# Cross-attention and a low-rank FFN: the value products on half chunks of 64 keys

## The chip, the cores and the metric

The kernel runs on one core of one Trainium2 chip. The metric is the device time of one execution in microseconds, as the median of several runs; lower is better. The kernel before takes 623.55 us (three runs, 623.04 to 624.56). One more execution, with the hardware profiler on, took 620.38 us.

## The reference

Everything is float32. `x` has shape (2, 2048, 512), `ctx` (2, 77, 384): 4096 tokens attend to only 77 keys of their own batch entry.

```
def _L0_xattn_ref(query, key_value, Wq, bq, Wk, bk, Wv, bv, Wo, bo):   # 16 heads of 32
    q = (query @ Wq + bq) -> (B, H, Nq, 32);  k, v likewise from key_value
    attn = jnp.einsum('bhqd,bhkd->bhqk', q, k) * 32 ** -0.5
    attn = jax.nn.softmax(jnp.clip(attn, -10000.0, 10000.0), axis=-1)
    x = jnp.einsum('bhqk,bhkd->bqhd', attn, v).reshape(B, Nq, 512)
    return x @ Wo + bo
def _L0_ffn_ref(x, U1, V1, b1, U2, V2, b2):                            # rank 128, 2048 hidden
    return gelu(x @ U1 @ V1 + b1) @ U2 @ V2 + b2
x = x + _L0_xattn_ref(_layernorm(x), ctx_768, ...)
x = x + _L0_ffn_ref(_layernorm(x), ...)
```

## The kernel before, in words

Each engine has its own instruction stream, ordered by hand; semaphores connect them. The attention stage goes over NA = 16 blocks of TA = 256 tokens, each of two tiles of 128 tokens (u = 0, 1); the blocks take turns between the two batch entries (b = 0, 1). The FFN stage goes over NB = 8 blocks of 512 tokens. The first blocks of a stage and its last are written out in the instruction streams, the ones between run in a hardware loop (`pairs`, `eng.Fori`).

Large projections split each float32 operand into a high part in fp32r and a low part, the rest, and add three products of the parts (`product`, L929). ScalarE writes the high part, VectorE or GpSimd subtracts to get the low one. The smaller products of attention are plain float32.

In one turn of the attention loop, block n is at several stages at once. TensorE's order for a turn (its `body`) is, for u = 0 and then u = 1: scores of block n (`scores`, L977); the turn of the probabilities of block n-1, first eight of the ten chunks of 128 (`turn_probs`, L1003); one half of the query projection of block n+1 (`project_q`); the last two chunks; the output projection of block n-2 (`project_out`). Then, once per block: the turn of the normalised input z of block n+2 (`turn_z`, L951) and the value products of block n-1 (`weigh_values`, L1026).

The softmax of a tile passes through four engines. VectorE clips the scores out of PSUM into a row buffer of 16 heads x 77 = 1232 values (`clip`, L717) and takes the maxima (L726). GpSimd subtracts them (`subtract_max`, L390), ScalarE takes the exponent (`exponent`, L527), VectorE the sums and reciprocals (`sums`, L731, L733), GpSimd multiplies (`normalise`, L397). Then TensorE turns the row in chunks of 128 into banks B5 and B6, and ScalarE copies them to `pt` (L520). There are four row buffers `sc`, two for each block.

A head's 77 keys lie across the 128-wide chunks at any offset. So the value products go by `PIECES`, the 25 overlaps of a head with a chunk. For each of them `vrows` holds a 128-row matrix that is zero outside the piece's rows, filled once by 25 small copies on SP's queue (L276) behind a memset. A product has 128 rows and 32 columns (one head); four heads share a bank by four column tiles. The heads of the first two groups end in B5, those of the other two in B6. After each half, `pv_full` lets ScalarE copy the high part to `ot` (`heads_high`, L533) and VectorE subtract the low part (`heads_low`, L739).

VectorE's order for a turn (its `body`, L822 on) is: for u = 0, 1: clip and maxima of block n; for u = 1 also the sums of tile 0; for u = 0 the two normalised z of block n+2 (`norm_z`, L661); the addition of the projected output to x (`y_sum`, L749); the statistics of block n+3 (L650, L653). Then the low parts of z (`turned_z`, L669), the sums of tile 1, the low parts of the heads of block n-1 (`heads_low`, L739). The first two blocks have an order of their own, `first_blocks` (L796). ScalarE's order ends a turn with the high parts of z (L489), the exponent of tile 1 and `heads_high`. GpSimd has normalise of tile 1 of the block before, subtract_max, two additions of a bias to x (L406), subtract_max, normalise, and a small power for the statistics (L368, L371).

`turn_z` used bank B6 for u = 0 and B4 or B7 for u = 1. `turn_probs` waits for `heads_low` (`ot_lo`), since B5 and B6 hold the value products before.

Of the kernel before, what the change touches and what calls it, by code (L numbers as in the profile page):

```python
# [4 lines left out]
F32 = mybir.dt.float32  # L5
# [5 lines left out]
P = 128  # L11
# [17 lines left out]
PIECES = [(h, c) for h in range(H) for c in range(NCH) if c * P < (h + 1) * KV and (c + 1) * P > h * KV]  # L29


def head_at(q):

    return (q % G) * GH + q // G


NP = len(PIECES)
# [35 lines left out]
def pairs(eng, total, body):  # L73

    head, tail = (2, 2) if total > 8 else (1, 1)
    for j in range(head):
        body(j)
    with eng.Fori(head, total // 2 - tail) as j:
        body(j)
    for j in range(total // 2 - tail, total // 2 + 1):  # L80
        body(j)


def xattn_ffn(nc, x, ctx, wq, bq, wk, bk, wv, bv, wo, bo, u1, v1, b1, u2, v2, b2, out):
# [7 lines left out]
    with stack:  # L92
# [3 lines left out]
        def sem(name):  # L96
# [27 lines left out]
        ss = sb("ss", [P, 4 * NCH * P])  # L124
        sc = ss[:, :].rearrange("p (s w) -> p s w", s=4)
# [5 lines left out]
        vrows = sb("vrows", [P, B, NP, DH])  # L131
# [8 lines left out]
        v_f = once[0:KV, KC * B * KV:KC * B * KV + B * D].rearrange("p (b d) -> p b d", b=B)  # L140
# [31 lines left out]
        z_bank = lambda j, b, u: B6 if u == 0 else B7 if is_block(2, j, b) or is_block(3, j, b) else B4  # L172
# [18 lines left out]
        wq_hi, wq_lo, wq_lo_pool, wo_hi, wo_lo, pad_zero, bias_ready = (  # L191
            sem(n) for n in ("wq_hi", "wq_lo", "wq_lo_pool", "wo_hi", "wo_lo", "pad_zero", "bias_ready"))
# [29 lines left out]

        def piece_rows(h, c):

            first, end = max(h * KV, c * P), min((h + 1) * KV, (c + 1) * P)
            return first - c * P, first - h * KV, end - first
# [18 lines left out]
        def _(sp):  # L245
# [85 lines left out]
            pairs(sp, NA, body)  # L331
# [17 lines left out]
            pairs(sp, NB, body2)  # L349
# [5 lines left out]
        def _(pool):  # L355
# [19 lines left out]
            pool.memset(vrows[:, :, :, :], 0.0).then_inc(zeroed, 1)  # L375
# [8 lines left out]
            def heads(t, k):  # L384
                return t[:, k, 0:HKV].rearrange("p (h w) -> p h w", h=H)
# [258 lines left out]
        def _(dve):  # L644
# [62 lines left out]
            for k in range(4):  # L707
                last = dve.memset(sc[:, k, HKV:], 0.0)
# [523 lines left out]
```

## Time and profile before

| | us |
|---|---|
| median of three runs | 623.55 |
| the profiled execution | 620.38 |
| its span, first to last instruction | 618.4 |
| TensorE busy | 582.5 (94%) |
| VectorE busy | 495.8 (80%) |
| GpSimd busy | 356.3 (58%) |
| ScalarE busy | 310.5 (50%) |
| attention stage, first scores to last output projection | 29 to 366 |

The profile has one row per instruction. Views of it add these up by line, by waits, along the chain of work that ended last, or list them in order of time. PE is TensorE's matmul, PEld its weight load, DVE VectorE, ACT ScalarE, POOL GpSimd, SP the queue of loads and stores. L1026 is line 1026 of the kernel. A float32 matmul that is not fp32r stands as two records. In the chain of waits a PE piece ends where the next begins; in the timeline the modelled end of a matmul reaches past the start of the next.

### The profile page before, as it was taken

How to read it: one execution, taken by the hardware profiler on the slowest of the kernel's cores; microseconds unless marked ns; L12 is line 12 of the kernel's file. 1: busy time of each engine (PE TensorE's matmuls, PEld its weight loads, DVE VectorE, ACT ScalarE, POOL GpSimd, SP SyncE). 2: the span in 40 equal slices, each digit the busy share in tenths (PEclk: the TensorE clock that was granted, in tenths of full speed). 3: DMA queues.
4: the chain of work that ended last, by engine and by line, in shares of the span. 5: the costliest groups of instructions: out<-in, count | busy, mean ns of one | idle time of the engine just before them, and what ended most of it. 6: DMA issues, size and time to landing. Idle time of an engine off the chain costs nothing.

```text
span 618.4 us, 12409 instructions
## 1 busy us (share of the span) xinstructions
PE 582.5 (94%) x4583; PEld 474.5 (77%) x4583; DVE 495.8 (80%) x706; ACT 310.5 (50%) x505; POOL 356.3 (58%) x250
## 2 busy tenths in 40 slices
PE   7886999999999999999998999898989898989996
PEld 6685887888888888888876677686868686868774
DVE  3589779889888888889679887988888888887664
ACT  1344354444544444535464546656565565656562
POOL 1549656665756665665556465646464738283641
PEclk9999999999999999999999999999999999999999
DMA  8423082303231223112320421212121111201012
GB/s 268 143 66 105 20 272 88 93 29 101 85 102 41 78 88 99 57 64 69 120 70 35 136 56 64 79 59 68 69 69 69 63 56 39 97 17 52 18 51 85
DMA packets 29733, 50.10 MB, mean 81 GB/s; under 512 B 5069, under 2 KB 6783, under 8 KB 29567
## 3 DMA queue, kind: packets, MB, share of 16 engines
q1 hardware_dynamic: 29215, 48.80, 23.8%
q10 hardware_dynamic: 480, 0.80, 0.5%
q8 instruction: 24, 0.39, 0.3%
q14 instruction: 14, 0.11, 0.1%
HBM read 32.49 MB, written 16.78 MB: 80 GB/s over the span
## 4 chain that ended last, share of the span: by engine, by line
PE 70%; DVE 13%; issue 5%; ACT 4%; POOL 3%; DMA 3%; SPq 1%; DVEq 0%; ACTq 0%; POOLq 0%
PE bank L929 40%; PE ps_s L929 10%; PE bank L1026 6%; PE bank L1003 5%; PE ps_s L977 4%; DVE once L770 3%; PE bank L1050 2%; DMA ss<-in_L_xattn_Wv 2%; DVE hs_r L791 2%; DVE hs_r L793 2%; DVE ssum L731 2%; PE bank L951 1%; DVE smax L726 1%; DMA xs<-in_x 1%; DVE ss L717 1%
## 5 line engine op out<-in xcount | busy, mean ns | idle before, releaser
L464 POOL TENSOR_TENSOR hs_r<-ss,hs_r 128x512 fp32r<-128x512 f32 x63 | 84.4, 1340 | 107.1 <-ACT hs_r L631 107.0
L610 ACT ACTIVATE ss<-ps_s,bias_c 128x512 f32<-128x512 f32 x128 | 88.1, 689 | 83.2 <-PE ps_s L929 80.2
L929 PE MATMUL bank<-hs_r,u_r 128*128 128x512 f32 x384 | 111.0, 398 | 14.0 <-DVE hs_r L793 10.5
L390 POOL TENSOR_TENSOR ss<-ss,smax 128x1232 f32<-128x1232 f32 x32 | 75.1, 2346 | 70.0 <-DVE smax L726 69.9
L929 PE MATMUL ps_s<-p1t_r,v_r 128*128 128x512 f32 x384 | 112.4, 401 | 0.7 <-DVE p1t_r L782 0.7
L929 PE MATMUL bank<-zt_r,wqo_r 128*128 128x256 f32 x768 | 99.5, 285 | 0.4 <-DVE zt_r L669 0.4
L929 PEld LDWEIGHTS bank<-hs_r,u_r 128*128 128x128 f32 x384 | 70.9, 188 | 36.4 <-DVE hs_r L793 8.8
L929 PE MATMUL bank<-wqo_r,ot_r 128*128 128x512 f32 x384 | 97.7, 403 | 0.2 <-DVE xs L749 0.2
L929 PEld LDWEIGHTS bank<-zt_r,wqo_r 128*128 128x128 f32 x768 | 93.2, 189 | 1.6 <-issue 1.0
L397 POOL TENSOR_TENSOR ss<-ss,rsum 128x1232 f32<-128x1232 f32 x32 | 72.1, 2253 | 38.6 <-DVE rsum L733 38.6
L929 PEld LDWEIGHTS bank<-wqo_r,ot_r 128*128 128x128 f32 x384 | 69.8, 188 | 15.6 <-issue 0.6
L929 PEld LDWEIGHTS ps_s<-p1t_r,v_r 128*128 128x128 f32 x384 | 69.8, 188 | 15.5 <-DVE v_r L756 1.1
L520 ACT ACTIVATE pt<-bank 128x512 f32<-128x512 f32 (+1 forms) x96 | 48.2, 526 | 43.1 <-PE bank L1003 43.1
L497 ACT ACTIVATE qt<-bank,bias_c 128x256 f32<-128x256 f32 x64 | 26.9, 472 | 70.0 <-PE bank L929 70.0
L793 DVE TENSOR_TENSOR hs_r<-ss,hs_r 128x512 fp32r<-128x512 f32 x64 | 59.7, 933 | 2.2
L791 DVE CAST hs_r<-ss 128x512 fp32r<-128x512 f32 x64 | 45.5, 710 | 14.7 <-ACT ss L610 14.6
L1003 PE MATMUL bank<-ident,ss 128*128 128x128 f32 x320 | 49.1, 281 | 8.4 <-DVE ot_r L739 2.4
L749 DVE TENSOR_TENSOR xs<-bank,xs 128x512 f32<-128x512 f32 x32 | 22.0, 687 | 40.9 <-PE bank L929 40.9
L1026 PE MATMUL bank<-pt,vrows 128*32 128x256 f32 x800 | 51.8, 383 | 0.0
L527 ACT ACTIVATE ss<-ss 128x1232 f32<-128x1232 f32 x32 | 39.5, 1234 | 24.4 <-POOL ss L390 24.4
L731 DVE TENSOR_REDUCE ssum<-ss 128x16 f32<-128x1232 f32 x32 | 45.7, 1429 | 2.1 <-ACT ss L527 2.1
L726 DVE TENSOR_REDUCE smax<-ss 128x16 f32<-128x1232 f32 x32 | 45.8, 1432 | 1.0
(89 smaller groups left out, 861.5 us busy)
## 6 DMA issues: line engine op xcount, KB each, us to landing
xs<-in_x SPq DMA_DIRECT2D x64, 256.0 KB, 2.8
y_between<-xs SPq DMA_DIRECT2D x32, 256.0 KB, 2.0
xs<-y_between SPq DMA_DIRECT2D x4, 1024.0 KB, 5.6
fw<-y_between SPq DMA_DIRECT2D x4, 1024.0 KB, 5.6
out<-fw SPq DMA_DIRECT2D x16, 256.0 KB, 2.0
out<-xs SPq DMA_DIRECT2D x16, 256.0 KB, 2.1
ss<-in_L_xattn_Wq SPq DMA_DIRECT2D x2, 512.0 KB, 10.3
xs<-in_L_xattn_Wo SPq DMA_DIRECT2D x1, 1024.0 KB, 10.9
```

Source lines behind the costliest of these rows:

```text
L390: pool.tensor_tensor(heads(sc, k), heads(sc, k), smax[:, k, :].unsqueeze(2).broadcast_to([P, H, KV]), ALU.subtract).then_inc(s_sub, 1)
L397: pool.tensor_tensor(heads(sc, k), heads(sc, k), rsum[:, k, :].unsqueeze(2).broadcast_to([P, H, KV]), ALU.mult).then_inc(s_norm, 1)
L464: pool.tensor_tensor(hs[:, c % 4, 1, :], hg[:, c % 4, :], hs[:, c % 4, 0, :].bitcast(F32), ALU.subtract)\
L520: act.activation(pt[:, c0:c0 + nch, u * P:(u + 1) * P], bk_[:, 0:nch * P].rearrange("p (c t) -> p c t", c=nch), ACT.Copy).then_inc(pt_copi ...
L610: act.activation(hg[:, c % 4, :], ps_s[:, c % 4, :], ACT.Gelu_apprx_tanh, bias=b1_c[:, c:c + 1]).then_inc(h_gelu, 1)
L726: dve.tensor_reduce(smax[:, k, :], heads(k), AX.X, ALU.max).then_inc(s_max, 1)
L731: dve.tensor_reduce(ssum[:, k, :], heads(k), AX.X, ALU.add).then_inc(s_sum, 1)
L791: dve.tensor_copy(hs[:, c % 4, 0, :], hg[:, c % 4, :]).then_inc(h_hi, 1)
L793: dve.tensor_tensor(hs[:, c % 4, 1, :], hg[:, c % 4, :], hs[:, c % 4, 0, :].bitcast(F32), ALU.subtract).then_inc(h_lo, 1)
L929: mm = pe.matmul(ps, lhs(a), rhs(c), start=first and i == 0, stop=last and i == len(PASSES) - 1)
L1003: last = pe.transpose(bk_[:, (c % 4) * P:(c % 4 + 1) * P], sc[:, k, c * P:(c + 1) * P], ident[:, :])
L1026: last = pe.matmul(bk_[d0:d0 + DH, i * TA:(i + 1) * TA], vrows[:, b, q, :], pt[:, c, :], start=first, stop=final)
```

## The change

The 77 keys of a head are cut into 64 and a tail of 13. `normalise` writes the probabilities in a new order into a buffer of its own (`sn`): first the 64 leading keys of each of the 16 heads, two heads to a chunk of 128; then, for four heads each, the last 16 keys of each, 64 to a half chunk. The 16 overlap the leading 64 by three keys, whose value rows are zero in the tail. So all of the ten chunks are full, and each half chunk of 64 rows is one piece: two pieces a head, 32 in all. Even chunks' halves go by row: rows 0 to 63 are one row tile, rows 64 to 127 the other, and the two write to B5 and B6. A product has 64 rows and 32 columns. The signal `pv_full` is given once, after all of them. `vrows` is filled by two large and eight small copies.

The two buffers `sn` take the place of two of the four row buffers, so that `clip` waits for the normalisation two tiles back and the normalisation for the turn two tiles back. z is turned in the score banks 0 and 1 from block 2 on, so `turn_z` waits for the clip and the scores for the low parts of z. The hardware loops are gone: all blocks of both stages are written out. The first GELU waits for the last normalisation. The padding of the row buffers and its memsets are gone.

```
-PIECES = [(h, c) for h in range(H) for c in range(NCH) if c * P < (h + 1) * KV and (c + 1) * P > h * KV]
+HALF = P // 2
+TAIL = HALF // GH
...
-def pairs(eng, total, body):
-    head, tail = (2, 2) if total > 8 else (1, 1)
-    for j in range(head):
-        body(j)
-    with eng.Fori(head, total // 2 - tail) as j:
-        body(j)
-    for j in range(total // 2 - tail, total // 2 + 1):
+def pairs(total, body):
+    for j in range(total // 2 + 1):
         body(j)
...
-        ss = sb("ss", [P, 4 * NCH * P])
-        sc = ss[:, :].rearrange("p (s w) -> p s w", s=4)
+        ss = sb("ss", [P, 2 * HKV + 2 * NCH * P])
+        sc = ss[:, 0:2 * HKV].rearrange("p (s w) -> p s w", s=2)
+        sn = ss[:, 2 * HKV:].rearrange("p (s w) -> p s w", s=2)
...
-        vrows = sb("vrows", [P, B, NP, DH])
+        vrows = sb("vrows", [P, 2, B, 2, GH, DH])
...
-        z_bank = lambda j, b, u: B6 if u == 0 else B7 if is_block(2, j, b) or is_block(3, j, b) else B4
+        z_bank = lambda j, b, u: (B6, B4)[u][:, :] if is_block(0, j, b) or is_block(1, j, b) else ps_s[:, u, :]
...
-            for q, (h, c) in enumerate(PIECES):
-                p0, kv0, n = piece_rows(h, c)
-                sp.dma_start(vrows[p0:p0 + n, :, q, :],
-                             v_f[kv0:kv0 + n, :, head_at(h) * DH:(head_at(h) + 1) * DH]).then_inc(v_placed, 16)
-                if q == NP // 2:
-                    load_x(2, 0)
+            for r in range(2):
+                sp.dma_start(vrows[r * HALF:(r + 1) * HALF, 0, :, :, :, :].rearrange("p b e i d -> p (b e i d)"),
+                             v_f[0:HALF, r, :, :, :].rearrange("p b e d -> p (b e d)")).then_inc(v_placed, 16)
+            load_x(2, 0)
+            v_heads = v_f.rearrange("p r b e (i d) -> p r (b e) i d", i=GH)
+            for r in range(2):
+                for i in range(GH):
+                    p0 = r * HALF + (i + 1) * TAIL - (KV - HALF)
+                    sp.dma_start(vrows[p0:p0 + KV - HALF, 1, :, :, i, :].rearrange("p b e d -> p (b e) d"),
+                                 v_heads[HALF:KV, r, :, i, :]).then_inc(v_placed, 16)
...
             def normalise(j, b, u):
-                k = 2 * b + u
-                pool.wait_ge(s_rec, 2 * num(j, b) + u + 1)
-                pool.tensor_tensor(heads(sc, k), heads(sc, k),
-                                   rsum[:, k, :].unsqueeze(2).broadcast_to([P, H, KV]),
+                k, s = 2 * b + u, 2 * num(j, b) + u
+                pool.wait_ge(s_rec, s + 1)
+                until(pool, pt_full, 3 * (s - 1))
+                pool.tensor_tensor(sn[:, u, 0:H * HALF].rearrange("p (h w) -> p h w", h=H), heads(u)[:, :, 0:HALF],
+                                   rsum[:, k, :].unsqueeze(2).broadcast_to([P, H, HALF]), ALU.mult)
+                grouped = lambda t: t.rearrange("p (i g) w -> p i g w", i=GH)
+                pool.tensor_tensor(sn[:, u, H * HALF:].rearrange("p (g i w) -> p i g w", g=G, i=GH),
+                                   grouped(heads(u)[:, :, KV - TAIL:KV]),
+                                   grouped(rsum[:, k, :].unsqueeze(2).broadcast_to([P, H, TAIL])),
                                    ALU.mult).then_inc(s_norm, 1)
...
             def heads_high(j, b):
                 n = 2 * j + b
+                act.wait_ge(pv_full, n + 1)
                 for half, bk_ in ((0, B5), (1, B6)):
-                    act.wait_ge(pv_full, 2 * n + half + 1)
...
             def clip(j, b, u):
-                until(dve, pt_full, 3 * (s - 3))
+                until(dve, s_norm, s - 1)
...
             def turn_z(j, b):
-                    if u == 0:
-                        if isinstance(j, int) and n < 3:
-                            until(pe, zt_lo, 2 * n - 1)
-                        else:
-                            pe.wait_ge(pt_copied, 6 * n - 13)
+                    if not (is_block(0, j, b) or is_block(1, j, b)):
+                        pe.wait_ge(s_clip, 2 * n - 2)
+                    elif u == 0:
+                        until(pe, zt_lo, 2 * n - 1)
...
             def scores(j, b, u):
+                if u == 0 and not is_block(0, j, b) and there(NA, j, b, 1):
+                    pe.wait_ge(zt_lo, 2 * n + 4)
...
             def weigh_values(j, b):
-                for half, bk_ in ((0, B5), (1, B6)):
-                    if half and (not isinstance(j, int) or n + 3 < NA):
-                        pe.wait_ge(zt_lo, 2 * (n + 3) + 1)
-                    for i in range(2):
-                        for head, q, c, first, final in value_steps(2 * half + i):
-                            d0 = head * DH
-                            last = pe.matmul(bk_[d0:d0 + DH, i * TA:(i + 1) * TA], vrows[:, b, q, :],
-                                             pt[:, c, :], start=first, stop=final)
-                    last.then_inc(pv_full, 1)
+                for e in range(2):
+                    for part in range(2):
+                        for i in range(GH):
+                            c = 2 * GH + e if part else 2 * i + e
+                            for r, bk_ in ((0, B5), (1, B6)):
+                                rows = slice(r * HALF, (r + 1) * HALF)
+                                last = pe.matmul(bk_[i * DH:(i + 1) * DH, e * TA:(e + 1) * TA],
+                                                 vrows[rows, part, b, e, i, :], pt[rows, c, :],
+                                                 start=part == 0, stop=part == 1)
+                last.then_inc(pv_full, 1)
```

## Rows read from the trace of the kernel before

**Rows 1.** The page: busy time of TensorE; the chain that ended last, by engine.

```profile
PE 582.5 (94%) x4583; PEld 474.5 (77%) x4583; DVE 495.8 (80%) x706; ACT 310.5 (50%) x505; POOL 356.3 (58%) x250
...
PE 70%; DVE 13%; issue 5%; ACT 4%; POOL 3%; DMA 3%; SPq 1%; DVEq 0%; ACTq 0%; POOLq 0%
```

**Rows 2.** Stretches: us, busy PE, PEld, DVE, ACT, POOL, granted clock, DMA share, GB/s.

```profile
138.23:158.34 20.11, 20.11 (x219) 17.04 (x222) 17.03 (x23) 9.15 (x17) 12.75 (x9) 1.00 0.25 78
...
279.07:299.22 20.15, 20.11 (x218) 17.09 (x222) 16.11 (x19) 9.08 (x17) 12.85 (x9) 1.00 0.17 53
```

**Rows 3.** The chain in order of time, block boundary at 138 us (start, us, what).

```profile
137.36 0.87 PE bank L951 x8
138.23 3.15 PE bank L1026 x50
141.38 1.06 PE ps_s L977 x32
142.45 1.20 PE bank L1003 x8
...
150.56 1.02 PE bank L1003 x8
```

**Rows 4.** Timeline of VectorE at the same boundary (start, us, line, operation, [idle before]).

```profile
137.40 0.69 DVE L749 TENSOR_TENSOR xs<-bank,xs 128x512 f32<-128x512 f32 x1 [1.93 <-PE bank L929]
138.00 0.68 DVE L650 BATCH_NORM_STATS2 stats<-xs 128x6 f32<-128x512 f32 x1
...
138.82 1.26 DVE L669 TENSOR_TENSOR zt_r<-bank,zt_r 128x512 fp32r<-128x512 f32 x2
...
140.07 1.44 DVE L731 TENSOR_REDUCE ssum<-ss 128x16 f32<-128x1232 f32 x1
...
141.71 1.22 DVE L739 TENSOR_TENSOR ot_r<-bank,ot_r 128x512 fp32r<-128x512 f32 x2
```

**Rows 5.** Timeline of ScalarE at the same boundary.

```profile
138.80 1.23 ACT L527 ACTIVATE ss<-ss 128x1232 f32<-128x1232 f32 x1
...
141.42 0.60 ACT L533 ACTIVATE ot_r<-bank 128x512 fp32r<-128x512 f32 x1 [0.68 <-PE bank L1026]
```

**Rows 6.** Waits from 118 to 299 us (engine, line, waited for: us, times, longest).

```profile
PEld bank L1003 <- DVE ot_r L739: 1.2, 7, 0.2
```

**Rows 7.** The chain near the start: the key-value projection, fp32, 512 columns a record.

```profile
16.07 2.80 PE bank L1066 x6
```

**Rows 8.** Timeline of GpSimd: normalise at the start and in a steady block.

```profile
46.48 2.25 POOL L397 TENSOR_TENSOR ss<-ss,rsum 128x1232 f32<-128x1232 f32 x1 [3.10 <-DVE rsum L733]
...
136.13 2.25 POOL L397 TENSOR_TENSOR ss<-ss,rsum 128x1232 f32<-128x1232 f32 x1
```

**Rows 9.** Groups of instructions on GpSimd (count, busy us, mean ns of one).

```profile
L406 POOL TENSOR_TENSOR xs<-xs,bias_row 128x512 f32<-128x512 f32 x32 | 45.2, 1432 | 0.3 <-DMA xs<-in_x 0.3
...
L368 POOL TENSOR_TENSOR var_e<-mv,eps_c 128x2 f32<-128x2 f32 x16 | 3.2, 198 | 15.2 <-DVE mv L653 15.2
```

**Rows 10.** Timeline of VectorE near the start.

```profile
41.24 1.43 DVE L717 TENSOR_SCALAR ss<-ps_s 128x1232 f32<-128x1232 f32 x1
...
44.67 1.44 DVE L731 TENSOR_REDUCE ssum<-ss 128x16 f32<-128x1232 f32 x1 [1.19 <-ACT ss L527]
...
48.42 1.41 DVE L717 TENSOR_SCALAR ss<-ps_s 128x1232 f32<-128x1232 f32 x1
...
49.75 3.84 DVE L661 TENSOR_SCALAR z<-xs,mv,rstd 128x512 f32<-128x512 f32 x2
```

**Rows 11.** The chain: the first turn of probabilities in the steady order.

```profile
61.63 1.16 PE bank L1003 x8
```

**Rows 12.** Timeline of SP's queue: the first 13 of the 25 value copies.

```profile
25.01 11.17 SPq L276 DMA_DIRECT2D vrows<-once  x13
```

**Rows 13.** The chain: the value products of the last block.

```profile
354.51 3.15 PE bank L1026 x50
```

**Rows 14.** Timeline of VectorE: the last low half of the heads.

```profile
358.33 0.69 DVE L739 TENSOR_TENSOR ot_r<-bank,ot_r 128x512 fp32r<-128x512 f32 x1 [0.59 <-ACT ot_r L533]
```

More of the change, by code:

```diff
@@ L374, in _ @@
             rstd_of(0, 0)
-            pool.memset(vrows[:, :, :, :], 0.0).then_inc(zeroed, 1)
+            pool.memset(vrows[:, 1, :, :, :, :], 0.0).then_inc(zeroed, 1)
             pool.wait_ge(wq_hi, 2)
@@ L603, in gelu @@
                 act.wait_ge(h_full, n + 1)
+                if is_block(0, j, b) and c == 0:
+                    act.wait_ge(s_norm, 2 * NA)
                 if not isinstance(j, int) or n >= 4:
@@ L676, in v_sum @@
                 dve.wait_ge(v_full, b + 1)
-                dve.tensor_tensor(v_f[:, b, :], (B5, B7)[b][0:KV, :], bias_row[0:KV, :],
+                halves = lambda t: t[0:KV, :].rearrange("p (e r d) -> p r e d", e=2, r=2)
+                dve.tensor_tensor(v_f[:, :, b, :, :], halves((B5, B7)[b]), halves(bias_row),
                                   ALU.add).then_inc(v_copied, 1)
@@ L705, in _, with heads @@
             v_sum(1)
-            for k in range(4):
-                last = dve.memset(sc[:, k, HKV:], 0.0)
-            last.then_inc(pad_zero, 1)
             turned_z(0, 1)
             def clip(j, b, u):
-                k, s = 2 * b + u, 2 * (2 * j + b) + u
+                s = 2 * (2 * j + b) + u
                 dve.wait_ge(s_full, s + 1)
-                until(dve, pt_full, 3 * (s - 3))
-                dve.tensor_scalar(sc[:, k, 0:HKV].rearrange("p (g w) -> p g w", g=G), ps_s[:, :, 0:GW],
+                until(dve, s_norm, s - 1)
+                dve.tensor_scalar(sc[:, u, :].rearrange("p (g w) -> p g w", g=G), ps_s[:, :, 0:GW],
                                   CLAMP, -CLAMP, ALU.min, ALU.max).then_inc(s_clip, 1)
-            def heads(k):
-                return sc[:, k, 0:HKV].rearrange("p (h w) -> p h w", h=H)
+            def heads(u):
+                return sc[:, u, :].rearrange("p (h w) -> p h w", h=H)
             def maxima(j, b, u):
@@ L959, in project_q @@
                     pe.wait_ge(q_done, 2 * n + 1)
-                elif is_block(2, j, b) or is_block(3, j, b):
-                    pe.wait_ge(q_done, 2 * n)
+                else:
+                    until(pe, q_done, 2 * n)
                 for i in range(2):
@@ L995, in turn_probs @@
                     elif part == 1 and u == 0:
-                        if isinstance(j, int) and n == 0:
-                            pe.wait_ge(zt_lo, 5)
-                        else:
-                            pe.wait_ge(ot_lo, 2 * n)
+                        until(pe, ot_lo, 2 * n)
                     elif part == 2:
@@ L1138, in body @@
                         if before:
-                            if isinstance(j, int) and num(j, b, -1) == 0 and u == 0:
-                                pe.wait_ge(pad_zero, 1)
                             turn_probs(*shift(j, b, -1), u, (0, 1))
```

75 lines of the change are left out of this document (29 added, 46 removed).

## The prediction

> **What bounds the kernel now.** The page's busy rows and the chain that ended last come first: TensorE is busy 94% of the span and holds 70% of the chain [rows 1]. Read alone, they say that a microsecond taken from TensorE is a microsecond of time. So the second view is the stage in which the change acts, cut at each start of the value products. From 77 to 299 us eleven blocks of 256 tokens take 20.1 us each, the mean within 0.1 of it; a looped one (138 us) and a written-out one (279 us) stand in [rows 2], TensorE busy nearly all of it at a granted clock of 1.00, VectorE 16 to 17 us. The page's busy share can't tell a TensorE that works from one whose next instruction begins just as its operand arrives, so I then read one boundary between blocks in order of time: TensorE's pieces in the chain [rows 3], VectorE's instructions [rows 4], ScalarE's [rows 5].
>
> At that boundary TensorE ends the output projection (137.36), turns z (0.87), weighs the values (3.15), makes the next scores (1.06) and turns the probabilities in 1.20 [rows 3]. The same eight transposes of the second tile take 1.02 [rows 3], where nothing holds them: about 0.2 us is a stall, and the waits name VectorE's subtraction into ot_r for it [rows 6]. That subtraction frees banks B5 and B6, into which the probabilities are turned. It is the last link of a strict line on VectorE that starts when the projection ends: y_sum at 137.40, statistics at 138.00, two low halves of z from 138.82, the sums at 140.07, a reciprocal, the two subtractions at 141.71, the last done at 142.93 [rows 4]. From the projection's end that is 5.57 us. TensorE's own work beside it, z + values + scores + half of the transposes, is 0.87 + 3.15 + 1.06 + 0.5 = 5.58 us [rows 3]. Both paths are as long as each other, and VectorE's is the one that already shows a stall. The value products are on the longer path by nothing.
>
> **The value products.** Before: 25 matmuls a block, two records each, 50 records in 3.15 us [rows 3]. An fp32 record of 512 columns takes 2.80 / 6 = 0.467 us [rows 7], so one of 256 about 0.23 us. The busiest of the four column tiles has 7 pieces, 14 records, 3.2 us: the products are bound by that tile. After: 32 matmuls, 64 records, on eight tiles, 4 pieces and 8 records each, 1.87 us if all eight run side by side. That 64-row and 32-column tiles do so no row shows. Two bounds: the eight-tile sum, 1.87 us, and the present rate without any gain from row tiles, 64 x 63 ns = 4.03 us. The scores run on four row tiles at 1.06 / 32 = 33 ns a record [rows 3], which gives 64 x 33 = 2.11 us. I take 2.11, the nearest row in kind and near the low end. TensorE saves 1.04 us a block.
>
> What the saving buys: TensorE reaches the transposes 1.04 us earlier and waits there for VectorE. The diff changes neither the order on VectorE nor the lengths in its line. Its start is the projection's end, and from the transposes' second part to the next projection TensorE has the same 14.5 us of work. So the cycle of 14.5 + 5.6 = 20.1 us stays, and **the saving is 0 in each of the blocks 2 to 13**. What must hold: the joined signal pv_full now comes after all products, not after each half. ScalarE's two copies of 0.60 start then [rows 5], VectorE's second subtraction of about 0.6 ends it. That last end is at 138.23 + D + 0.04 + 1.20 + 0.04 + 0.65 (0.04 is the hand-off from 141.38 to 141.42 [rows 3, 5]) = 140.16 + D. It stays hidden behind 142.93 while D, the length of the products, is under 2.77 us. At 2.11 there are 0.66 us in hand. ScalarE's exponent (138.80, 1.23) ends at 140.03 [rows 5], before the products do.
>
> A rule of the Trainium skill speaks against the change: "TensorE: Matmul & The Clock Gate", section "The mechanism" of Part 3, says that weight loads overlap running matmuls only where the row group differs. With two row groups that would leave two matmuls at a time, and 7.4 us of products. The trace of before disagrees: all its pieces have one row group and 50 records of 0.23 us fit into 3.15 us, over three at once. I give the rule the small chance below.
>
> **The waits that are added.** (a) z is turned in score banks 0 and 1, so the next scores wait for both low halves of z. They end at 140.08 [rows 4]; the products would end at 138.23 + 2.11 = 140.34. Nothing, and even late scores have the 1 us stall behind them. turn_z waits for the clip of the second tile, which can start when the scores before 150.56 [rows 3] are done and takes 1.4 us, five before turn_z at 157.4: nothing. (b) clip waits for the normalisation two tiles back, since there are two score buffers where there were four. In the steady blocks that normalisation (136.13, 2.25 long [rows 8]) is done by 138.4 and its clip starts at 142.9: nothing. Behind clip on VectorE the whole line would queue. (c) The normalisation waits for the transposes two tiles back, one half block of TensorE's work, 150.56 - 142.45 = 8.1 us [rows 3], before: nothing.
>
> **The normalisation** becomes two instructions over 1280 elements instead of one over 1232. At 2.25 us / 1232 = 1.83 ns an element [rows 8] that is 0.09 us more, and a second instruction costs at most the 0.20 us of a two-element one [rows 9]: +0.3 us. Bounds: 0, and the rate of the slowest plain addition, 1432 ns / 512 = 2.8 ns [rows 9], which makes 3.58 us, +1.3. The tail is read and written in runs of 16 in another order; no row shows such a pattern. I take 0.3, since the present instruction has broadcast operands in short runs too. In steady blocks it ends 4 us before its transposes, so all of it is hidden there.
>
> **The start** is where it shows. Up to 61.63 us VectorE and GpSimd hand work back and forth in series, and the first full transposes wait for that [rows 10, 11]. The clip at 48.42 now waits for the normalisation that started at 46.48 [rows 8, 10] and comes after another one in the same line: it can start at 48.73 + 2 x 0.3 = 49.33, 0.9 later. The two z instructions behind it take 3.84 us for 512 elements each [rows 10] because GpSimd's instructions hold them, and those move only by 0.6. So +0.6 (0.6 to 0.95; with the upper price 2.9). The scores of block 1 wait now for z of block 2, some 3 us; the clip moves from 41.24 to 42.5, and VectorE had 1.19 us idle before its sums at 44.67 [rows 10], which takes it. The value copies fall from 25 issues to 10; 13 took SP's queue 11.17 us [rows 12]. All 25 were through by 25.01 + 25 x 0.86 + the 1 us of a load between them, before the tile normalised until 48.73 can even be turned for the first products: nothing. The memset and the padding sit beside idle time: nothing.
>
> **The end of the stage.** After block 16's values (354.51 [rows 13]) there is no line on VectorE; the projection starts when the subtraction of 358.33 is over, 359.02 [rows 14]. With the products done at 356.62 it ends at 356.62 + 0.04 + 1.20 + 0.04 + 0.69 = 358.59: -0.4 us. At 299 to 340 us ScalarE or GpSimd releases the transposes: 0.
>
> **Loops written out.** Blocks inside the hardware loop and written out have one period, 20.11 against 20.15 [rows 2]: neither a loop cost to win nor a code-loading cost to fear that shows. 0.
>
> **Sum.** 618.4 + 0.6 - 0.4 + 12 x 0 = 618.6 of span; the profiled run has 620.38, so 1.98 around it, 620.6. The runs' median is 3.17 above the profiled one: **623.7 us**. About 0.3%, 1.9 us, is what a measurement can tell from no change.
>
> **The rivals.**
> - *TensorE is the bound after all.* The saving passes through: 13 x 1.04 + 0.4 = 13.9, less 0.6: 610.3 us. For it: the busy rows and the 70%. Against it: the two equal paths above and the stall on ot_r. 10%.
> - *Written-out waits shorten VectorE's line.* Its seven hand-offs have some 0.04 us each; if all went, 12 x 0.28 = 3.4 us: 620.3. Against: the written-out blocks of before don't show it. 8%.
> - *GpSimd's re-ordering is dear.* At +1.3 us a normalisation the clip at 48.42 waits till 51.3 (+2.9), and the one that releases the last block's transposes near 340 us adds 1.3; less 0.4: 627.2 us. It decides from about +0.9 a normalisation; in steady blocks even 4 us stay hidden. For it: the untried pattern. Against: no row near it is dear. 13%.
> - *Row tiles don't run side by side.* D = 4.03 us puts the last subtraction at 144.19, 1.26 late in each of 13 blocks, and 0.9 at the end: 623.55 + 0.6 + 16.4 + 0.9 = 641.5 us. It decides from D = 2.77. Against: the scores' four row tiles take 33 ns a record, where one 77-column record by itself would take 77 / 512 x 467 = 70 ns. 7%.
> - *Loads wait for their row group.* Two records at a time are 64 x 0.23 / 2 = 7.4 us, 4.6 late in 13 blocks: 684 us. This is the skill's rule named above. 2%.
>
> **How the numbers follow.** The forecast has 60%, its own range 621.5 to 625.5. Leaving out the first and the last two rivals leaves out 19%, so the range reaches from the small gain to past the dear re-ordering: 618 to 629. Faster by over 0.3%: 10 + 8 + 2 of the forecast's own spread = 20%. Slower: 13 + 7 + 2 + 1 of the spread = 23%. Within: 57%.
>
> **What would show it.** Right: value products of about 2.1 us a block, and behind the scores a TensorE stall of 1.0 to 1.2 us on ot_r in every steady block, periods of 20.1 as before; the first full transposes at 62.2; a normalisation of 2.5 us. Wrong: periods under 19.8 (then VectorE's line started or ended earlier than I have it), products over 2.8 us with the copies of ScalarE right behind them, or a clip that waits on GpSimd outside the start.

## The result, and the profile after

The changed kernel takes 627.29 us (median of four runs, 625.49 to 627.67), the kernel before 624.05 us in the four runs beside it (623.04 to 624.61). The ratio is 1.006, with an interval of 1.0033 to 1.0086: slower by 3.2 us, about 0.5%. (Ratios and intervals are given as recorded; they are not the quotients of the two medians.) The forecast was 623.7 us. The profiled execution took 625.49 us, its span is 623.7 us, 5.3 us longer than that of before. Of the experiments below, one run each of the two kernels with a new VectorE order, at 1922 and 659 us, is disturbed and left out of the ratios, though not of the medians.

On the page TensorE is busy 10 us less than in [rows 1], in a span that is longer. It holds 64% of the chain where it held 70%, and VectorE has gone from 13% to 18%.

```profile
PE 572.1 (92%) x4807; PEld 472.4 (76%) x4807; DVE 491.7 (79%) x702; ACT 308.0 (49%) x505; POOL 364.0 (58%) x282
...
PE 64%; DVE 18%; issue 5%; POOL 5%; ACT 3%; DMA 3%; SPq 1%; POOLq 0%; DVEq 0%; ACTq 0%
```

Three stretches of the changed kernel, each from one first turn of probabilities to the next (columns as in [rows 2]):

```profile
145.17:165.24 20.07, 18.84 (x229) 16.16 (x229) 16.93 (x23) 8.97 (x16) 13.29 (x11) 1.00 0.26 85
165.24:186.85 21.61, 20.37 (x229) 17.69 (x229) 16.93 (x23) 8.93 (x16) 13.31 (x11) 0.92 0.23 74
186.85:206.93 20.08, 18.84 (x229) 16.18 (x229) 16.94 (x23) 8.97 (x16) 13.29 (x11) 1.00 0.24 79
```

The first and the third are what was forecast: the period of [rows 2], with TensorE busy 1.3 us less in it. The second has the same instructions and the same VectorE time, and takes 1.5 us more at a granted clock of 0.92. TensorE's timeline across the boundary between the first two:

```profile
159.95 1.03 PE L937 MATMUL ps_s<-ident,z 128*128 128x128 f32 x8
160.91 1.96 PE L1002 MATMUL bank<-pt,vrows 64*32 64x256 f32 x64
162.97 1.13 PE L965 MATMUL ps_s<-kt,qt 32*128 32x77 f32 x32
165.24 1.31 PE L988 MATMUL bank<-ident,ss 128*128 128x128 f32 x8 [1.13 <-DVE ot_r L730]
166.20 4.56 PE L920 MATMUL bank<-zt_r,wqo_r 128*128 128x256 f32 x24
```

The products take 1.96 us, the transposes behind the scores wait 1.13 us for VectorE's `ot_r`, and then the 24 matmuls of half a query projection take 4.56 us. VectorE's line beside it is that of [rows 4] to 0.02 us, piece by piece:

```profile
160.15 0.69 DVE L740 TENSOR_TENSOR xs<-bank,xs 128x512 f32<-128x512 f32 x1 [1.97 <-PE bank L920]
...
161.57 1.25 DVE L662 TENSOR_TENSOR zt_r<-ps_s,zt_r 128x512 fp32r<-128x512 f32 x2
162.82 1.44 DVE L722 TENSOR_REDUCE ssum<-ss 128x16 f32<-128x1232 f32 x1
...
164.46 1.22 DVE L730 TENSOR_TENSOR ot_r<-bank,ot_r 128x512 fp32r<-128x512 f32 x2
```

Windows of 1 us over the same place (same columns; the granted clock is the third number from the end):

```profile
165.00:166.00 1.00, 0.77 (x6) 0.68 (x7) 1.00 (x3) 0.10 (x1) 1.00 (x1) 1.00 0.90 340
166.00:167.00 1.00, 1.00 (x8) 1.00 (x7) 1.00 (x1) 0.92 (x2) 1.00 (x2) 0.55 0.61 176
167.00:168.00 1.00, 1.00 (x6) 1.00 (x6) 0.96 (x2) 0.18 (x1) 0.13 (x1) 0.50 0.08 23
...
169.00:170.00 1.00, 1.00 (x8) 1.00 (x8) 1.00 (x1) 0.00 (x0) 1.00 (x1) 0.74 0.00 0
```

TensorE is at the lower of its two levels, 1.2 instead of 2.4 GHz, just behind its wait, while it is busy. In the chain the price is read off one pair of pieces, the first half projection of the block without the fall and of the block with it: 4.22 - 2.83 = 1.4 us.

```profile
146.33 2.83 PE bank L920 x24
...
166.54 4.22 PE bank L920 x24
```

Such falls stand in the changed kernel's trace at 12 to 16, 43 to 46, 63 to 67, 166 to 169, 248 to 251, 309 to 312 and 330 to 333 us. The trace of before has a granted clock of 1.00 in all of its 1 us windows up to 617 us. In the steady blocks its transposes waited 0.2 us [rows 6]. (It did have longer waits elsewhere, of 1.8 to 2.1 us at 41, 49 and 62 us and of 1.8 us at 427 us, and no fall behind them.) Here the waits between 110 and 300 us (total, times, longest) say:

```profile
PE bank L988 <- DVE ot_r L730: 10.2, 9, 1.1
```

Every block waits, and behind some of the waits, not all, the clock goes down.

Where the 5.3 us of span come from, by the offsets of the same piece after and before: +0.9 at the first normalisation, 0.6 of it with the fall at 12 to 16 us (the 24 matmuls of the key projection take 5.06 us in the chain below, 3.39 before; a later profile of the same kernel without this fall has +0.3 there); +1.38 at the first transposes in the steady order (63.01 against [rows 11]); +2.90 at 105 us, +2.69 at 165, +4.19 at 187, +4.04 at 247, +5.43 at 269, +6.74 at the last value products. The end of the stage gives back 0.8, and the rest up to 5.3 comes back behind it, which I have not followed. A steady block without a fall gives back up to 0.1 us; a fall adds 1.4 to 1.5.

```profile
11.26 5.06 PE ps_s L1071 x24
```

### The profile page after: what moved, and what is told of

It is laid out like the page before. It is cut to its first block, busy times and chain, and to the rows that moved or that the text cites. A ratio compares the mean times of both kernels' runs of the same rounds, so it can differ in the third digit from the quotient of the medians.

```text
span 623.7 us, 12020 instructions
## 1 busy us (share of the span) xinstructions
PE 572.1 (92%) x4807; PEld 472.4 (76%) x4807; DVE 491.7 (79%) x702; ACT 308.0 (49%) x505; POOL 364.0 (58%) x282
## 4 chain that ended last, share of the span: by engine, by line
PE 64%; DVE 18%; issue 5%; POOL 5%; ACT 3%; DMA 3%; SPq 1%; POOLq 0%; DVEq 0%; ACTq 0%
PE bank L920 42%; PE ps_s L920 10%; PE bank L988 6%; DVE ssum L722 4%; DVE once L761 3%; PE ps_s L965 2%; DVE zt_r L662 2%; PE bank L1027 2%; DVE ot_r L730 2%; DVE hs_r L784 2%; DMA fw<-in_L_xattn_Wk 1%; DVE stats L643 1%; DVE hs_r L782 1%; POOL ss L378 1%; DMA xs<-in_x 1%
## 5 line engine op out<-in xcount | busy, mean ns | idle before, releaser
L920 PE MATMUL bank<-zt_r,wqo_r 128*128 128x256 f32 x768 | 105.4, 296 | 0.4 <-DVE zt_r L662 0.4
L920 PEld LDWEIGHTS bank<-zt_r,wqo_r 128*128 128x128 f32 x768 | 99.3, 201 | 1.6 <-issue 1.0
L386 POOL TENSOR_TENSOR ss<-ss,rsum 128x1024 f32<-128x1024 f32 x32 | 61.4, 1919 | 37.8 <-DVE rsum L724 37.7
L988 PE MATMUL bank<-ident,ss 128*128 128x128 f32 x320 | 50.8, 291 | 19.2 <-DVE ot_r L730 17.9
L988 PEld LDWEIGHTS bank<-ident,ss 128*128 128x128 f32 x320 | 36.8, 146 | 25.0 <-issue 19.6
L782 DVE CAST hs_r<-ss 128x512 fp32r<-128x512 f32 x64 | 43.6, 681 | 15.4 <-ACT ss L603 15.2
L708 DVE TENSOR_SCALAR ss<-ps_s 128x1232 f32<-128x1232 f32 x32 | 45.7, 1428 | 2.6 <-PE ps_s L965 2.5
```

The lines of the kernel that those rows point to most:

```text
L386: pool.tensor_tensor(sn[:, u, 0:H * HALF].rearrange("p (h w) -> p h w", h=H), heads(u)[:, :, 0:HALF], rsum[:, k, :].unsqueeze(2).broadcast ...
L708: dve.tensor_scalar(sc[:, u, :].rearrange("p (g w) -> p g w", g=G), ps_s[:, :, 0:GW], CLAMP, -CLAMP, ALU.min, ALU.max).then_inc(s_clip, 1)
L782: dve.tensor_copy(hs[:, c % 4, 0, :], hg[:, c % 4, :]).then_inc(h_hi, 1)
L920: mm = pe.matmul(ps, lhs(a), rhs(c), start=first and i == 0, stop=last and i == len(PASSES) - 1)
L988: last = pe.transpose(bk_[:, (c % 4) * P:(c % 4 + 1) * P], sn[:, u, c * P:(c + 1) * P], ident[:, :])
```

## The experiments

All were timed in five rounds beside the kernel before, whose medians in the three groups were 622.79, 623.73 and 623.59 us (23 to 29 runs each). The idle times and the places of falls that are given without a line are read from the same views as those shown, of each run's own trace.

**The wait filled in the steady blocks.** If the idle wait is what costs the clock, idle work in it must bring the clock back and change nothing else.

```
@@ turn_probs(j, b, u), part 0, ahead of the wait
+    if u == 0 and not is_block(NA - 1, j, b):
+        for i in range(9):
+            pe.transpose(B4[:, 0:P], ident[:, :], ident[:, :])
     pe.wait_ge(s_norm, s + 1)
```

> The changed kernel with nine idle transposes of the identity into bank B4 (about 0.11 us each) ahead of the first turn of the probabilities of each block, where TensorE waits 1.1 us for VectorE. Theory A (the period is VectorE's, and the 1.1 us of waiting is what lets the granted clock fall to 1.2 GHz for some 3 us, at about 1.4 us a fall): periods stay at 20.1 us, the falls from 63 us on are gone, time 620 to 622. Rival B (the falls come with the value products on eight tiles, not with the wait): the falls stay, 626 to 628. Rival C (TensorE's own work sets the period): 1.0 us longer in 13 blocks, 640.

Measured: 620.65 us, ratio 0.9963 (0.9936 to 0.999). The chain of waits in the same block as above:

```profile
145.08 1.13 PE ps_s L965 x32
146.21 1.13 PE bank L978 x9
...
147.35 1.16 PE bank L991 x8
148.51 2.85 PE bank L920 x24
```

The nine idle transposes fill exactly the 1.13 us, the period is 20.09 us, and between 110 and 600 us there is no fall; two at the start are left (42 to 49 and 62 to 69 us). The kernel does more work than the changed one and is faster.

**The wait made on the kernel before**, by less work in the products: only the first piece of each head, 16 of 25; part of the keys is left out.

```
@@ value_steps
-    for k in range(max(len(m) for m in mine)):
+    for k in range(1):
...
-            yield head, *m[k], k == 0, k == len(m) - 1
+            yield head, *m[k], True, True
```

> The kernel before, with only the first piece of each head weighed: 16 value products instead of 25, the output lacks the rest of the keys. No row tiles, no new order of the probabilities, loops as before. Theory A: products about 1.9 us, the turn of the probabilities waits 1.2 us on ot_r in each block, period 20.1 as before, and the clock falls now and then as in the changed kernel: 623 to 629. Rival B (falls come with eight tiles): no falls, 622.5 to 624. Rival C (TensorE is the bound): 13 x 1.2 us less, 609.

Measured: 621.98 us, ratio 0.997 (0.995 to 0.9989). Two of its chain's first turns, and what leads to the first:

```profile
143.09 0.64 DVE ot_r L739
...
143.78 1.25 PE bank L1003 x8
...
163.94 1.25 PE bank L1003 x8
```

The period is 20.16 us, though TensorE has more than 1 us less to do: TensorE is not the bound. Part of the freed time stands inside the products, as a wait of 0.3 us on the low half of z, and only 0.7 to 0.8 us in one piece before the transposes, up to 300 us. So the wait that I wanted on this kernel came out shorter than that of the changed one; up to 300 us it brought no fall, and the time is below the 623 to 629 us expected. Its last two waits in the stage are longer, 1.14 us at 305 and 1.59 us at 324 us, and behind the second the clock falls, where the kernel before waits 0.8 us and has no fall:

```profile
324.37 2.33 PE L1003 MATMUL bank<-ident,ss 128*128 128x128 f32 x10 [1.59 <-DVE ot_r L739]
```

```profile
325.00:326.00 1.00, 1.00 (x6) 0.77 (x4) 1.00 (x1) 0.60 (x1) 1.00 (x1) 0.50 0.00 0
```

This one fall speaks for the theory that the wait costs the clock; alone it does not show it.

**VectorE's line made shorter, after and before.** The sums of the second tile and one of the statistics go behind the low halves of the heads, so that 2.1 us (1.44 and 0.68) and the small instructions beside them leave the line that ends in `ot_r`. The same edit on both kernels.

```
@@ VectorE's body
-                        if there(NA, j, b, 3):
-                            norm_stats(*shift(j, b, 3), u)
+                        if there(NA, j, b, 3) and u == 0:
+                            norm_stats(*shift(j, b, 3), 0)
...
-                    if here and not is_block(NA - 1, j, b):
+                    late = here and there(NA, j, b, 2)
+                    if here and not late and not is_block(NA - 1, j, b):
                         sums(j, b, 1)
...
                         heads_low(*shift(j, b, -1))
+                    if late:
+                        sums(j, b, 1)
+                    if there(NA, j, b, 3):
+                        norm_stats(*shift(j, b, 3), 1)
```

> The changed kernel, with VectorE's sums of tile 1 and its statistics for tile 1 moved behind the two low halves of the heads (2.5 us out of the line between the projection and the turn of the probabilities). Theory A: the line is then the products, two copies on ScalarE, one subtraction: the wait shrinks from 1.1 to about 0.4 us, periods of 19.2 to 19.3, fewer falls of the clock: 611 to 615. If VectorE's line is not the bound: 626 to 628.

> The kernel before with the same move on VectorE. Theory A: TensorE's own 19.94 us a block become the bound, only the stall of 0.2 us goes: 621 to 622.5. If the move by itself is what helps (rival D), it gains as much here as in the changed kernel: 611 to 615.

Measured, on the changed kernel: 613.69 us, ratio 0.9835 (0.98 to 0.987). On the kernel before: 622.14 us, ratio 0.9982 (0.9959 to 1.0004). The chain of the changed kernel with it:

```profile
138.98 1.97 PE bank L1007 x64
...
140.97 0.60 ACT ot_r L525
...
141.60 0.70 DVE ot_r L730
...
142.44 1.17 PE bank L993 x8
```

and that of the kernel before with it:

```profile
142.94 1.06 PE ps_s L982 x32
144.00 1.02 PE bank L1008 x8
...
163.97 1.02 PE bank L1008 x8
```

Before, only the stall of 0.2 us goes, and the period is 19.97 us, all TensorE. After, it is 19.28 us, 0.69 less: the products save 1.18 and 0.5 of it is still a wait; that wait on `ot_r` is 0.5 us, held by the products' own end, and no block up to 300 us has a fall (one comes at 317 us, behind a wait of 1.59). So the products' saving is real, and VectorE's line was what hid it.

**The changed kernel again**, beside the next two. No edit.

> The changed kernel once more, as the measure for the three beside it. 624 to 628, with two to six falls of the granted clock after 60 us, each 1.4 us, so a wider spread than a kernel without them.

Measured: 625.80 us, ratio 1.0034 (1.0013 to 1.0056). The falls in its profile stand at 60 to 67, 105 to 108, 228 to 231, 309 to 313 and 330 to 333 us: four behind the waits of the later blocks as before, two of them elsewhere, and none at 12 and 43 us. Its twelve runs have granted clocks of 0.975 to 0.989.

**Four column tiles in place of eight tiles**, as long and with the same wait. One bank's half is left out, and heads are mixed.

```
@@ weigh_values
-                            for r, bk_ in ((0, B5), (1, B6)):
-                                rows = slice(r * HALF, (r + 1) * HALF)
-                                last = pe.matmul(bk_[i * DH:(i + 1) * DH, e * TA:(e + 1) * TA],
-                                                 vrows[rows, part, b, e, i, :], pt[rows, c, :],
+                                last = pe.matmul((B5, B6)[e][i * DH:(i + 1) * DH, 0:TA],
+                                                 vrows[:, part, b, e, i, :], pt[:, c, :],
```

> The changed kernel with 16 value products of 128 rows on four column tiles instead of 32 of 64 rows on eight; one bank half is left out and heads are mixed, so the output is not attention's. By the 0.23 us a record and 8 records a tile the products take the same 1.9 to 2.0 us, so the wait on ot_r is the same 1.1 us. Theory A (the wait lets the clock fall): as the changed kernel beside it, within 1.5 us. Rival B (the eight tiles let it fall): 4 to 7 us faster than that one, no falls in the steady blocks.

Measured: 625.89 us, ratio 1.004 (1.0018 to 1.0061). TensorE's timeline:

```profile
163.18 1.93 PE L1001 MATMUL bank<-pt,vrows 128*32 128x256 f32 x32
165.24 1.13 PE L965 MATMUL ps_s<-kt,qt 32*128 32x77 f32 x32
167.50 1.16 PE L988 MATMUL bank<-ident,ss 128*128 128x128 f32 x8 [1.13 <-DVE ot_r L730]
```

The same wait and the same time as the changed kernel beside it, and falls at four of the same places (64, 228, 310, 330 us). So the 64-row tiles are not needed for the falls.

**The row tiles one after the other.** All products of rows 0 to 63, then those of rows 64 to 127.

```
@@ weigh_values
-                for e in range(2):
-                    for part in range(2):
-                        for i in range(GH):
-                            for r, bk_ in ((0, B5), (1, B6)):
+                for r, bk_ in ((0, B5), (1, B6)):
+                    for e in range(2):
+                        for part in range(2):
+                            for i in range(GH):
```

> The changed kernel with the same 32 products, all of the first row tile before all of the second. If the two row tiles run side by side in the changed kernel, this takes twice the length: 3.7 to 3.9 us instead of 1.96. The last subtraction then ends 140.16 + 3.8 - 142.93 = 1.0 us later than before: periods of 21.1, and the line has no long wait of TensorE: 634 to 638. If not (the loads or the issue set the 1.96 us): as the changed kernel.

Measured: 624.14 us, ratio 1.0006 (0.9984 to 1.0028). That is far from what I expected:

```profile
161.50 2.85 PE L1002 MATMUL bank<-pt,vrows 64*32 64x256 f32 x64
...
165.88 1.16 PE L988 MATMUL bank<-ident,ss 128*128 128x128 f32 x8 [0.47 <-DVE ot_r L730]
```

The products take 2.85 us, not 3.7 or more: one after the other, the row tiles still get through a record in 45 ns. Side by side they take 31 ns, so the order gives 30% and not a half. Why it is 2.85 stays open. But the run is worth more for something else. Its products are 0.9 us longer than those of the changed kernel and it is no slower (its interval lies mostly below): with the wait down to 0.5 us, no block up to 300 us has a fall.

**Other banks for the first turn**, on top of the shorter line: the turn of tile 0 goes to B7, B5, B6 and waits for each bank by itself.

```
@@ turn_probs, and the copies to pt
-                    bk_ = (B5, B6, B5)[part]
+                    bk_ = ((B7, B5, B6), (B5, B6, B5))[u][part]
...
-                            pe.wait_ge(ot_lo, 2 * n)
+                            until(pe, y_done, 2 * n - 2)        # part 0: B7
+                    elif part == 1 and u == 0:
+                        until(pe, ot_lo, 2 * n - 1)             # B5
                     elif part == 2:
+                        if u == 0:
+                            until(pe, ot_lo, 2 * n)             # B6
```

> The reordered kernel, and in addition the first four chunks of tile 0 are turned into bank B7 (free once y_sum is done), the next four into B5, the last two into B6, so that the turn waits for VectorE's halves one step later. Theory A: the last 0.5 us of waiting in each block goes, periods of 18.8 to 18.9 us, TensorE's own sum: 606 to 609. If something else holds the reordered kernel at 19.28 us (GpSimd's or ScalarE's line): 612 to 615.

Measured: 606.01 us, ratio 0.973 (0.9702 to 0.9759). The chain:

```profile
139.21 1.89 PE bank L1009 x64
141.10 1.06 PE ps_s L970 x32
142.16 1.08 PE bank L995 x8
...
157.91 1.89 PE bank L1009 x64
```

In the steady blocks there is no wait left: TensorE works through, with a period of 18.70 us. From 20.11 that is 1.4 us a block: the products' 1.2, and the 0.2 of the stall. The falls in its profile stand at 42 to 49, 62 to 69 and 319 to 322 us, the last behind a wait of 1.56.

**The hardware loops put back** on every stream but TensorE's attention.

```
-def pairs(total, body):
-    for j in range(total // 2 + 1):
-        body(j)
+def pairs(eng, total, body):
+    head, tail = (2, 2) if total > 8 else (1, 1)
...
+    with eng.Fori(head, total // 2 - tail) as j:
+        body(j)
```

> The changed kernel with the hardware loops back on every engine and in both stages, but for TensorE's attention stream, which stays written out. Theory A (loops cost nothing that shows): as the changed kernel, 1.000 to 1.006 of the kernel before, periods of 20.07. Rival (the longer code is fetched late, or the loops' register waits cost VectorE's line): more than 2 us off the changed kernel on either side.

Measured: 626.79 us, ratio 1.0037 (1.0016 to 1.0058), as the changed kernel (1.0034 beside its own group): no cost and no gain of the written-out blocks shows.

**The wait filled everywhere**, at the start too: 28 idle transposes ahead of the scores of block 1, 24 ahead of its turn, 9 in later blocks.

```
+            def idle(n):
+                for i in range(n):
+                    pe.transpose(B4[:, 0:P], ident[:, :], ident[:, :])
@@ scores
+                if is_block(1, j, b) and u == 0:
+                    idle(28)
@@ turn_probs, part 0
+                        if u == 0 and n < NA - 1:
+                            idle({0: 0, 1: 24}.get(n, 9))
```

> The changed kernel with idle transposes in all its long waits up to 310 us: 28 ahead of the scores of block 1 (a wait of 3.2 us), 24 ahead of the turn of block 1's probabilities (2.7 us), 9 in each later block (1.1 us). Theory A: no fall of the clock between 40 and 320 us in most runs, about 1.5 to 2 us less for each fall of the changed kernel: 617.5 to 619.5. If the falls come from elsewhere: 624 to 627.

Measured: 619.87 us, ratio 0.9946 (0.9926 to 0.9967), just above the 617.5 to 619.5 expected. The kernel with the loops, which runs as the changed one, took 626.79 us in the same group: idle work alone is worth 6.9 us. Its profile in two windows, the projections at the start and all that follows up to 600 us:

```profile
11.00:16.00 5.00, 4.61 (x22) 4.64 (x23) 1.23 (x1) 1.06 (x1) 0.00 (x0) 0.66 1.06 379
16.00:600.00 584.00, 558.77 (x4871) 461.08 (x4870) 479.28 (x680) 299.98 (x495) 359.68 (x269) 1.00 0.23 77
```

**The same at the start of the kernel before**: 16, 18 and 16 idle transposes in its three long waits there.

```
@@ turn_probs, part 0
+                        if isinstance(j, int) and s == 1:
+                            pe.wait_ge(q_done, 5)
+                        if isinstance(j, int) and s in (0, 1, 2):
+                            idle((16, 18, 16)[s])
```

> The kernel before with 16, 18 and 16 idle transposes in its three waits of 1.8 to 2.1 us at 39, 47 and 60 us. Theory A: its median lies 3 us over its profiled run (which had no fall after 40 us) because most runs have one or two falls there. So 620.3 to 621.5 and a narrower spread. Rival: the profiler's run is faster for another reason: 623 to 624.

Measured: 622.65 us, ratio 0.9979 (0.9961 to 0.9996): a gain of 0.9 us, less than I expected. The profiled run has falls at 13 to 16 and 429 to 433 us only. Neither is touched by this edit. The second stands in the FFN stage, behind a wait that the edit leaves as it was:

```profile
428.77 1.40 PE L929 MATMUL bank<-hs_r,u_r 128*128 128x512 f32 x3 [1.80 <-DVE hs_r L793]
```

The two variants of the kernel before above, with fewer products and with the shorter line, have a fall behind the same wait; the profiled run of the kernel before has the wait, at 427 us, and no fall. So there are places with falls that I had not thought of. How much of the missing gain they are isn't shown.

**All together**: other banks, shorter line, and 28, 7 and 10 idle transposes in the three waits at the start.

```
@@ on top of the other banks
+                if is_block(1, j, b) and u == 0:
+                    idle(28)                                    # scores
...
+                            if n == 1:
+                                idle(7)                         # turn, part 0
+                        if n == 1:
+                            idle(10)                            # turn, part 1
```

> The reordered kernel with the other banks, and idle transposes in the waits of the first blocks: 28, 7 and 10. Theory A: the falls at 43 and 63 us go, 2 x 1.5 to 2 us: 602 to 603.5. If not: 606.

Measured: 603.69 us, ratio 0.9686 (0.9662 to 0.9709), just above the 602 to 603.5 expected, 3.1% faster than the kernel before and the fastest of all. Behind the fall at 11 to 14 us its profile has none up to 590:

```profile
15.00:590.00 575.00, 549.15 (x4781) 453.65 (x4781) 465.23 (x685) 302.91 (x501) 360.82 (x271) 1.00 0.24 79
```

## Why the prediction was right, and where it wasn't

**The equal paths: right.** The saving on TensorE became a wait for VectorE's line, block by block: 1.13 us where 1.0 to 1.2 were forecast, and periods of 20.07. Three experiments show that it is this line: less work on the kernel before leaves the period at 20.16; the line shortened brings it to 19.28 after and only to 19.97 before; without the wait it is 18.70.

**The products: right.** 1.96 us against 2.11, between the bounds, near the sum over eight tiles (1.87). The rival in which row tiles don't run side by side is refuted, and so is the one in which loads wait for their row group: 64 records in 1.96 us. By the rule weighed in the prediction ("TensorE: Matmul & The Clock Gate" of the Trainium skill, "The mechanism" of Part 3) they would take 7.4 us, an estimate that takes the rule as two matmuls at a time; the trace doesn't agree with it, not even where one row group stands for 16 products in a row (2.85 us for both groups).

**The normalisation: right.** Two groups of the view by line and form:

```profile
L386 POOL TENSOR_TENSOR ss<-ss,rsum 128x1024 f32<-128x1024 f32 x32 | 61.4, 1919 | 37.8 <-DVE rsum L724 37.7
...
L389 POOL TENSOR_TENSOR ss<-ss,rsum 128x256 f32<-128x256 f32 x32 | 22.3, 697 | 0.0
```

1.92 + 0.63 to 0.70 us, +0.3 to 0.4 where 0.3 was forecast; the re-ordering isn't dear. The rival built on it had 627.2 us (its own terms, 623.55 + 2.9 + 1.3 - 0.4, make 627.35), the time that came, and the wrong mechanism: a right number shows nothing until its place in the trace is found.

**The start: right, where no fall is in the way.** In the profile of the changed kernel again there is no fall before 60 us, and the path is the one forecast. The first normalisation starts 0.3 us later than in the kernel before (39.18 against 38.91), for a reason that I have not followed. Behind the second one, GpSimd and VectorE:

```profile
48.87 0.63 POOL L389 TENSOR_TENSOR ss<-ss,rsum 128x256 f32<-128x256 f32 x1
```

```profile
49.61 1.44 DVE L708 TENSOR_SCALAR ss<-ps_s 128x1232 f32<-128x1232 f32 x1 [0.58 <-POOL ss L389]
```

The clip waits for the normalisation and starts 1.2 us after that of [rows 10], 0.9 without the 0.3 ahead; the first full transposes come at 62.40, 0.8 after [rows 11], 0.5 without it, for the 0.6 forecast. The new wait of the scores is absorbed, as forecast. In the first profile of the changed kernel it isn't:

```profile
42.35 0.91 PE L965 MATMUL ps_s<-kt,qt 32*128 32x77 f32 x24 [3.19 <-DVE zt_r L662]
...
63.01 1.48 PE L988 MATMUL bank<-ident,ss 128*128 128x128 f32 x8 [2.65 <-DVE ot_r L730]
```

There the clip starts at 50.26, behind the second tile's scores and 0.15 us after the normalisation (50.11): the half clock behind the 3.19 us wait made TensorE as late as GpSimd. Taken off the 0.9 us at the first normalisation, the first full transposes are late by the same 0.5 us. What an idle TensorE does to the clock was not asked.

**The end: right sign, twice the size.** The products after block 16 start 6.74 us later than [rows 13], the output projection behind them 5.96 later: a gain of 0.8 us for the 0.4 forecast.

```profile
361.25 1.97 PE bank L1002 x64
...
365.21 1.90 PE bank L920 x7
```

**The step that failed: "the saving is 0 in each of the blocks 2 to 13".** The sum over the steps was 0.2 us, and 3.2 us were measured. The term that was mis-sized is the price of the new wait itself. A wait of 1.1 us isn't neutral here: it precedes falls of the granted clock to half, each 1.4 to 1.5 us of the chain. Filled with idle work, the wait has its length and the falls are gone, with 6.9 us of time (this takes in the waits at the start); made by another kind of products, it brings the same falls; cut to 0.5 us in two different ways, it brings none up to 300 us. That the wait costs the clock is thereby shown. The counts behind it, up to 300 us: 7 falls at 44 waits of 1.0 to 1.1 us in four profiled runs (the changed kernel twice, four tiles, loops), none at 33 waits of 0.5 to 0.8 us in three, none at the 22 filled ones. From 300 us on, the waits of 1.3 and 1.6 us of the same four runs had a fall behind each, and so had the one of 1.59 us with fewer products and with the shorter line. Other waits as long had none: 1.56 us at 314 us with all together, and those of 1.8 to 2.1 us in the profiled run of the kernel before. Why a fall comes behind one wait and not behind another of the same length isn't shown.

Nor is the time inside the range by merit alone. It lies outside the forecast's own range of 621.5 to 625.5, among the slower outcomes that had 23% together, and none of the reasons given for them came true. The wide range held it by the room left for a dear re-ordering: that is luck.

**The 3.17 us carried over as a constant** were of the same kind. The span of before's runs goes with their granted clock: in the first group of experiments 618.2 to 618.6 us at 0.997 to 0.999, mostly 620.4 to 621.2 at 0.991, 622.3 to 624.4 at 0.989 to 0.985. Not all fit: one run at 0.949 has 620.1 us, and runs at 0.994 lie between 620.5 and 622.5. The profiled run had no fall up to 617 us; that the others have one, two or three, at some 2 us each, is my reading of these means, since they have no trace. For the changed kernel the same difference is 1.8 us, not 3.17, so here the carried constant was 1.4 us too large and hid a part of the error: the profiled run was forecast at 620.6 us and took 625.49. The difference between a profiled run and the median was the clue in hand, and I passed it by.

**Rivals.** TensorE as the bound is refuted by the kernel with fewer products (20.16 us a block), and written-out waits that shorten the line by the hardware loops put back (626.79 us) and by VectorE's timeline.

## What to carry to other kernels

Time taken from an engine that waits at the end of another's line becomes a wait, and on TensorE the wait can cost more than nothing, so a saving there should go in together with the cut to the other line (here -2.7% with both and other banks, +0.6% alone) or with idle work in the gap. Look at the granted clock behind every wait that a change lengthens, the ones at the start too. And where the profiled run is faster than the median, look whether its granted clock is higher, before the difference is added to a forecast as a constant.

## What the runs showed of the hardware

- The granted clock fell behind waits as short as 1.0 us (105 us in the changed kernel again), and the 24 matmuls of a half projection took 4.22 us in place of 2.83. The falls came in three or four of the later blocks of a run; the places partly repeat (about 229, 311 and 331 us in three kernels). Waits of 1.8 to 2.1 us in the profiled run of the kernel before had no fall behind them: a wait does not fix it alone. The Trainium skill ("TensorE: Matmul & The Clock Gate", "A second HAM failure mode: psum-queue depth-cycling") tells of short idle times between groups of matmuls that make the clock swing; the traces agree.
- Idle transposes of the identity, 0.125 us each (9 in 1.13 us), hold the clock. The same page of the Trainium skill ("Part 4: PE-mode transpose") says that transposes don't count as busy in the same way; here, between matmuls, they were enough: no fall from 16 to 600 us with them.
- 64-row, 32-column tiles took 31 ns a record with the two row groups in turn, 45 ns with one group after the other; 32 records of 128 rows on four column tiles took 1.93 us, 60 ns each, near the 63 of the pieces in [rows 3].
